# Tile transposes placed singly between the matmuls of the next step, instead of four in a row at a step's end

## The reference

```python
f = jax.nn.relu(jnp.einsum('bld,ldf->bf', x, W_enc) + b_enc)    # W_enc 2 x 1024 x 4096
x_hat = jnp.einsum('bf,lfd->bld', f, W_dec) + b_dec             # W_dec 2 x 4096 x 1024
```

## Time and profile before

| what | us |
|---|---|
| time, median of 3 runs (661.69 to 661.98) | 661.72 |
| time of the profiled execution | 662.01 |
| its span, first to last instruction | 660.2 |
| TensorE busy with matmuls (2892) | 644.7 |
| of this the 192 transposes | 26.3 |
| VectorE busy | 572.0 |
| ScalarE busy | 337.4 |

### The profile page before, as it was taken

The page is one execution under the profiler, slowest core; times in us unless marked ns, Lnnn a source line. Parts: engine busy times, 40 slices in busy tenths (PEclk is TensorE's granted clock), DMA queues, the critical chain, the costliest instruction groups (busy, mean ns, idle before and its releaser), DMA issues.

```text
span 660.2 us, 8023 instructions
## 1 busy us (share of the span) xinstructions
PE 644.7 (98%) x2892; PEld 524.8 (79%) x2892; DVE 572.0 (87%) x752; ACT 337.4 (51%) x425; POOL 17.3 (3%) x25
## 2 busy tenths in 40 slices
PE   6899999999999999999999999999999999999996
PEld 3777888888887888888888888788877888888885
DVE  6999989879999856659897599999999999998854
ACT  4555335354565445455665657545555445464452
POOL 0110000000000000000000000001100011011000
PEclk9899999999999999999999999999999999999999
DMA  8985564654465464545545465559955579689625
GB/s 328 388 240 192 192 216 167 222 198 152 160 206 182 170 218 165 190 150 187 177 154 196 139 230 191 189 211 252 275 187 192 191 227 279 197 215 310 209 96 188
DMA packets 43958, 135.81 MB, mean 206 GB/s; under 512 B 5136, under 2 KB 5136, under 8 KB 43920
## 3 DMA queue, kind: packets, MB, share of 16 engines
q1 hardware_dynamic: 40896, 125.87, 54.5%
q0 software_dynamic: 2736, 8.91, 7.3%
q10 hardware_dynamic: 288, 0.52, 0.2%
HBM read 122.18 MB, written 4.19 MB: 191 GB/s over the span
## 4 chain that ended last, share of the span: by engine, by line
PE 81%; DVE 14%; issue 2%; ACT 1%; DMA 1%; DVEq 0%; SPq 0%; ACTq 0%
PE sums L632 27%; PE sums L634 26%; PE sums L633 26%; DVE w_split L408 6%; DVE w_raw L408 3%; PE sums L646 3%; DVE forms L408 2%; DVE s_sum L408 2%; DVE place L408 1%; DMA w_raw<-w_enc 1%; ACT w_split L291 0%; ACT place L331 0%; ACT place L344 0%; ACT w_split L358 0%; ACT forms L309 0%
## 5 line engine op out<-in xcount | busy, mean ns | idle before, releaser
L291 ACT CAST w_split<-w_raw 128x1024 fp32r<-128x1024 f32 (+1 forms) x255 | 239.6, 945 | 288.8 <-PE sums L634 202.7
L632 PE MATMUL sums<-w_split,forms 128*128 128x512 f32 x896 | 354.8, 396 | 9.2 <-DVE w_split L408 7.6
L634 PE MATMUL sums<-w_split,forms 128*128 128x512 f32 x896 | 350.1, 391 | 0.0
L633 PE MATMUL sums<-w_split,forms 128*128 128x512 f32 x896 | 349.5, 390 | 0.0
L408 DVE TENSOR_TENSOR w_split<-w_raw,w_split 128x1024 fp32r<-128x1024 f32 (+1 forms) x257 | 269.0, 1082 | 60.8 <-ACT w_split L291 59.6
L632 PEld LDWEIGHTS sums<-w_split,forms 128*128 128x128 f32 x896 | 168.6, 188 | 51.9 <-issue 13.5
L634 PEld LDWEIGHTS sums<-w_split,forms 128*128 128x128 f32 x896 | 168.5, 188 | 36.2
L633 PEld LDWEIGHTS sums<-w_split,forms 128*128 128x128 f32 x896 | 168.8, 188 | 33.6
L408 DVE TENSOR_TENSOR w_raw<-w_raw 128x512 f32<-128x512 f32 x252 | 173.4, 688 | 6.9 <-DMA w_raw<-w_dec 2.6
L408 DVE TENSOR_TENSOR place<-place,sums 128x1024 f32<-128x1024 f32 (+1 forms) x26 | 29.5, 1175 | 5.9 <-PE sums L634 3.7
L408 DVE TENSOR_TENSOR forms<-s_sum,forms 128x512 fp32r<-128x512 f32 x48 | 32.9, 685 | 0.2
(11 more groups left out here) (23 smaller groups left out, 66.3 us busy)
## 6 DMA issues: line engine op xcount, KB each, us to landing
w_raw<-w_dec SPq DMA_DIRECT2D x96, 512.0 KB, 4.2
w_raw<-w_enc SPq DMA_DIRECT2D x94, 512.0 KB, 4.2
w_raw<-w_enc SPq DMA_DIRECT2D x36, 256.0 KB, 2.8
w_raw<-w_dec SPq DMA_DIRECT2D x32, 256.0 KB, 2.9
place<-place POOLq DMA_DIRECT2D x15, 512.0 KB, 8.6
place<-xT SPq DMA_DIRECT2D x8, 512.0 KB, 9.5
outT<-place SPq DMA_DIRECT2D x14, 256.0 KB, 2.2
w_raw<-w_raw POOLq DMA_DIRECT2D x4, 256.0 KB, 7.0
```

The source lines that it names most:

```text
L291: nc.scalar.copy(split(s, q, 0), w_pos(s, 2 * q, n)).then_inc(hi_done, 1)
L632: nc.tensor.matmul(out, v_hi, w_hi, start=k == 0 and n != UNBROKEN + 1, stop=False)
L633: nc.tensor.matmul(out, v_lo, w_hi, start=False, stop=False)
L634: last = nc.tensor.matmul(out, v_hi, w_lo, start=False, stop=k == PAIRS - 1 and n != UNBROKEN)
```

## The change

In chunks 5, 6, 7 and 8 the transposes of a tile no longer stand at the end of step k, but inside `multiply` of step k + 1: one after the first matmul and one after the second matmul of each (p, m), until the tiles of that step are done. A step of one tile so has M T M T M, M T M T M in product 0 (M a matmul, T a transpose), a step of two tiles has the same in product 1 as well. The steps with transposes become 2, 3, 4, 5 (one tile each) and 6, 7 (two each). The waits and the signal of a tile stay at its first and its last transpose. In chunk 15 (`woven` is false for the last chunk) the order stays as it was.

```diff
-            def multiply(s, products, rows=(0, 1), signal=True):
+            def multiply(s, products, rows=(0, 1), signal=True, tiles=()):
+
+                done = 0
...
                         nc.tensor.matmul(out, v_hi, w_hi, start=k == 0 and n != UNBROKEN + 1, stop=False)
+                        if done < 4 * len(tiles):
+                            transpose_block(n - 1, tiles[done // 4], done % 4)
+                            done += 1
                         nc.tensor.matmul(out, v_lo, w_hi, start=False, stop=False)
+                        if done < 4 * len(tiles):
+                            transpose_block(n - 1, tiles[done // 4], done % 4)
+                            done += 1
                         last = nc.tensor.matmul(out, v_hi, w_lo, start=False,
                                                 stop=k == PAIRS - 1 and n != UNBROKEN)
...
+            def transpose_block(n, j, b):
+
+                t = TILED.index(n + 1) * 8 + j
+                if b == 0:
+                    if t == 0:
+                        pe.wait_ge(ident_set, 2)
+                    if j == 0:
+                        pe.wait_ge(summed, SUMMED[n + 1])
+                    if t >= 2:
+                        pe.wait_ge(tile_out, t - 1)
+                transpose(n, j, 6 + t % 2, [b], b == 3)
...
+                woven = n in TILED and n < len(CHUNKS) - 1
                 if s < STEPS - 2:
-                    multiply(s, range(4 if FOUR[s] else 3))
+                    multiply(s, range(4 if FOUR[s] else 3),
+                             tiles=[j for j in range(8) if woven and TILE_STEP[j] + 1 == k])
...
-                if n in TILED:
+                if n in TILED and not woven:
                     for j in range(8):
                         if TILE_STEP[j] == k:
-                            t = TILED.index(n) * 8 + j
-                            if t == 0:
-                                pe.wait_ge(ident_set, 2)
-                            if j == 0:
-                                pe.wait_ge(summed, SUMMED[n])
-                            if t >= 2:
-                                pe.wait_ge(tile_out, t - 1)
-                            transpose(n - 1, j, 6 + t % 2)
+                            for b in range(4):
+                                transpose_block(n - 1, j, b)
```

## The result

Measured: 664.03 us (663.21 to 664.80, 6 runs) against 661.92 of the kernel before (661.69 to 663.47, 6 runs); ratio 1.0027, 95% interval 1.0015 to 1.0039. The change makes the kernel slower: by 2.1 us or 0.32% by the medians, by 0.27% by the ratio, which takes in all executions; 663.4 was predicted, from 661.4 to 665.0. The profiled execution took 663.21, with a span of 661.4, 1.2 above that of the kernel before.

What follows compares the result with a forecast made beforehand. TensorE was taken as the bound, every transpose lying on the path that sets the end. Terms +0.74 - 0.30 + 0.42 + 0.81 = +1.67 took the profiled 662.01 to 663.68, median 663.4 us, range 661.4 to 665.0.

Steps and rivals of the forecast that it cites:

- A transpose costs the same singly, but for the slow matmuls (+0.74): Chunks 5 to 8, TensorE: single transposes expose as many loads as rows; 168 more slow matmuls x 0.0044 give +0.74 us.
- 42 slow matmuls in a chunk: Extra slow matmuls: 5 more in a step of one tile, 11 in a step of two, 4 x 5 + 2 x 11.
- Both bounds: Limits on the slow-matmul term: below, the slowness vanishes, gain 1.05 us; above, 104 more breaks x 0.043, +4.5 us.
- Why: On TensorE a load starts one matmul ahead at most; behind a transpose it is bared, so whatever follows starts 0.11 us later.
- The first rival: Weight loads hide, so each transpose costs only its columns, 0.057 us; 654.9 us, chance 0.06.
- Chunks 6 and 7 (-0.30): At these chunk starts TensorE's wait for two of the four `take_out` on VectorE goes: -0.30 us for both.
- Chunk 8 (+0.42): Chunk 8's start: `hi` behind a double tile on ScalarE comes 0.43 later, so does the `take_out` TensorE awaits: +0.42 us.
- Chunk 9 (+0.81): `copy_out(8, 0)` waits for the last transpose of F, now in product 1; the wait of chunk 9's product 2 grows by 0.81 us.
- Sum: All terms, +0.74 - 0.30 + 0.42 + 0.81 = +1.67 us, giving a median of 663.4 against 661.72.

Runs made afterwards that it cites:

- the 64-column matmuls: Changed kernel with a bf16 matmul of zeros, 64 moving columns, in place of each transpose of F; 0.13 us each, one-tile step 0.547 us over its 18 matmuls.
- the last run: Against the kernel before: rows of eight, chunk 7's last two tiles later on ScalarE, step 64's low forms behind both `lo` of step 65; 660.34 us, ratio 0.9970.

## Why the prediction was right, and where its terms were off

- **A transpose costs the same singly, but for the slow matmuls (+0.74).** Right in kind. In the steps of one tile 0.507 us over 18 matmuls, in the two steps of two tiles 0.988 and 0.972, in chunk 6 with all that follows 4.00 / 32 = 0.125 each, against 0.117: +0.92 over the four chunks by the timelines, and 0.67 by the run that put the rows at the same late place. The 0.25 between them is the row of eight broken in two, which that run has as well; the prediction's count of 42 slow matmuls in a chunk took the two together. Both bounds were far off: the slowness did not vanish, and single transposes did not each pay a whole tail.
- **Why.** That a single small matmul costs 0.11 or more whatever it streams is shown by the 64-column matmuls; that it is the load of the matmul behind is read from the order of the loads. That loads also set the pace of four in a row is not shown: half the load columns changed nothing. Both prices are about 0.11 here, so the sum did not suffer. The first rival, that a transpose costs only its columns, 0.057, is dead by the same runs.
- **Chunks 6 and 7 (-0.30).** Right: the first matmul of chunk 6 comes at its pace, and by the timelines the two chunk starts gained 0.14 and 0.15.
- **Chunk 8 (+0.42).** The way was right: the second tile ahead of `hi` on ScalarE, `hi` 0.32 late, the `take_out` 0.30. The hole grew by 0.20 (0.39 to 0.59).
- **Chunk 9 (+0.81).** The way was right: putting chunk 8 back takes the loss away, and the wait is read in ScalarE's timeline. The hole grew by 0.60. Both terms were mis-sized by the same row: 0.47 from a fourth transpose to its tile was taken for the delay of the signal, but ScalarE was busy with a `hi` until then. Where it waits, it starts 0.31 after the last transpose (370.92 to 371.23). With 0.16 less the terms are 0.26 and 0.65. That `hi`, of the kernel before, stands right ahead of the tile at 234.89:

```profile
234.36 0.62 ACT L291 CAST w_split<-w_raw 128x512 fp32r<-128x512 f32 x1 [0.31 <-PE sums L634]
```

- **Sum.** The parts give 0.92 - 0.29 + 0.20 + 0.57 = 1.40 (0.57 is the hole with its tail), and chunks 5 to 9 grew by 1.39; the prediction's sum was 1.67. That the median grew by 2.1 is no credit to it: the rest lies in stretches that it did not look at, of which the profiles show chunk 14.

## What to carry to other kernels

In this kernel a small matmul between long ones cost 0.11 us at the least, even where its columns stream in 0.03, and the records put this on the weight load of the long one behind it. Spreading transposes hides their own load and bares another; rows of eight are the cheaper form, 3.64 / 32 = 0.114 each over chunk 6 of the last run against 0.125, since a break has a price of its own. A result that another engine waits for should not come later for the sake of the order on the engine that makes it; a wait in the next chunk, by way of `copy_out` for the last transpose, cost 0.57, not far from the 0.67 of the single places themselves. And a signal's delay is to be read where the receiver is idle.

## What the runs showed of the hardware

- After a break on TensorE, by a transpose or a wait, up to ten 512-column matmuls come every 0.231 us before the pace is 0.2267 again, at a full granted clock in the windows above; behind some breaks it is only two. What slows them stays open.
- A transpose of 64 rows between matmuls of 128 rows cost 0.41 instead of 0.125: neither its load nor the next one started ahead.
- A row of fp32 transposes of 128 columns kept its pace of 0.108 with half the weight columns.
- The weight load of a bf16 matmul between fp32r matmuls did not begin with the matmul ahead of it, as a transpose's load does, but 0.23 later, when the small matmul itself began.
